# Attention stage: spread and scores as four products on 32 rows each, x loaded a unit ahead, inverse norms placed in one instruction

## The reference

```python
h = concat(patch_embedding(x), text_embedding_with_layer_norm(x_txt, ...))     # (64, 93, 192)
h = h + attn(layernorm(h));  h = h + ffn(layernorm(h))

# attn: 12 heads of 64
w = (x @ w_qkv) per head                                  # (64, 12, 93, 64)
w_normed = w / max(sqrt(sum over tokens of w*w), 1e-12)
logits = sum(w_normed * w_normed, -1) * temp              # (64, 12, 93)
Pi = softmax(logits);  Pi_norm = Pi / (sum(Pi) + 1e-8)
dots = sum over tokens of Pi_norm * (w * w)               # (64, 12, 64)
out = -(w * Pi) * 1/(1 + dots);  return out @ w_out + b_out

# ffn: 8 groups of 16 codes, 64 experts each, the best 4 are taken
z = x @ P;  scores = z @ C.T per group;  top 4, softmax over them
h = gelu(z @ W1 + b1);  yl = h @ W2 + b2;  comb = sum of yl by weight
return gelu(comb @ G1 + g1b) @ G2 + g2b
```

## Time and profile before

| | |
|---|---|
| time, median of 2 runs | 1391.95 us (1391.14 to 1392.76) |
| profiled execution | 1391.86 us, of which the span of the trace is 1390.1 us |
| stage 1, stage 2, stage 3 | 0 to 122 us, 122 to 627 us, 627 to 1390 us of the span |
| busy over the span | PE 88%, DVE 79%, ACT 78%, POOL 72% |

### The profile page before, as it was taken

One profiled execution on the slowest core, in us unless ns is written; L12 is line 12 of the kernel. 1 busy time (PEld: TensorE's weight loads), 2 busy tenths in 40 slices (PEclk: granted clock), 3 DMA queues, 4 the chain that ended last, 5 costly groups with the idle time before them and its releaser, 6 DMA issues.

```text
span 1390.1 us, 34218 instructions
## 1 busy us (share of the span) xinstructions
PE 1228.7 (88%) x12232; PEld 625.1 (45%) x12232; DVE 1104.9 (79%) x3371; ACT 1086.3 (78%) x2696; POOL 995.5 (72%) x712
## 2 busy tenths in 40 slices
PE   2953799999999999858999999999999999999996
PEld 2941466666666666522343333333343333333332
DVE  5592488888888888957888888888888888888884
ACT  0244467777677767539999999999999999999994
POOL 7641367756776676617888888888888888788884
PEclk7975899999999999969999999999999999999998
DMA  9564313222222222134214222232413323232410
GB/s 268 152 136 81 59 34 100 63 69 74 95 72 67 73 92 69 51 86 108 64 44 89 65 70 64 57 70 54 101 41 87 69 59 64 56 77 53 95 38 12
DMA packets 95705, 107.06 MB, mean 77 GB/s; under 512 B 12772, under 2 KB 92668, under 8 KB 95254
## 3 DMA queue, kind: packets, MB, share of 16 engines
q1 hardware_dynamic: 86576, 94.95, 26.3%
q10 hardware_dynamic: 6848, 6.13, 2.6%
q0 software_dynamic: 2112, 3.79, 1.1%
HBM read 67.88 MB, written 33.71 MB: 73 GB/s over the span
## 4 chain that ended last, share of the span: by engine, by line
PE 21%; ACT 18%; DVE 12%; issue 3%; POOL 0%; POOLq 0%; DVEq 0%
DVE arena L1474 11%; ACT ring L1073 11%; PE ring L1736 9%; PE code L1749 9%; ACT arena L1085 6%; PE ring L1768 2%; PE ring L1759 1%; DVE arena L1482 0%; ACT arena L1081 0%; POOL arena L817 0%; POOLq L157 0%; PE ring L1586 0%; PE ring L1634 0%; DVE arena L1257 0%; DVEq L1473 0%
## 5 line engine op out<-in xcount | busy, mean ns | idle before, releaser
L1474 DVE TENSOR_TENSOR arena<-ring,arena 128x496 f32<-128x496 f32 x1008 | 611.4, 668 | 123.4 <-ACT ring L1073 123.4
L817 POOL TENSOR_TENSOR arena<-arena 128x992 f32<-128x992 f32 x264 | 611.7, 2330 | 121.1 <-ACT arena L1085 111.6
L1073 ACT ACTIVATE ring<-ring 128x496 f32<-128x496 f32 x1008 | 544.9, 688 | 16.9 <-PE ring L1736 16.0
L1736 PE MATMUL ring<-arena,w_stack 99*32 99x496 bf16 x6144 | 423.9, 375 | 23.5 <-DVE arena L1474 17.7
L1749 PE MATMUL code<-arena,w_pad 128*32 128x496 f32 x3072 | 389.6, 581 | 8.3 <-DVE arena L1482 8.0
L1736 PEld LDWEIGHTS ring<-arena,w_stack 99*32 99x32 bf16 x6144 | 163.5, 95 | 399.6 <-DVE arena L1474 220.3
L1085 ACT ACTIVATE arena<-ring 128x992 f32<-128x992 f32 x252 | 283.9, 1127 | 0.7 <-PE ring L1736 0.7
L1578 PE MATMUL ring<-arena 96*128 96x372 f32 x384 | 135.3, 490 | 1.5 <-ACT arena L929 0.9
L1749 PEld LDWEIGHTS code<-arena,w_pad 128*32 128x32 f32 x3072 | 97.5, 110 | 59.6 <-DVE arena L1474 22.5
L753 POOL TENSOR_TENSOR arena<-arena 128x372 f32<-128x372 f32 x96 | 91.9, 986 | 32.7 <-DVE arena L1314 32.7
L1578 PEld LDWEIGHTS ring<-arena 96*128 96x128 f32 x384 | 71.7, 194 | 62.3 <-ACT arena L937 15.9
(11 more groups left out here) (143 smaller groups left out, 1437.1 us busy)
## 6 DMA issues: line engine op xcount, KB each, us to landing
arena<-gates SPq DMA_DIRECT2D x48, 496.0 KB, 6.7
gates<-arena SPq DMA_DIRECT2D x16, 744.0 KB, 11.5
arena<-h_scratch SPq DMA_DIRECT2D x32, 279.0 KB
arena<-z_parts SPq DMA_DIRECT2D x144, 62.0 KB, 2.7
h_scratch<-arena SPq DMA_DIRECT2D x16, 279.0 KB
z_parts<-arena SPq DMA_DIRECT2D x48, 93.0 KB, 2.1
arena<-h_scratch SPq DMA_DIRECT2D x12, 372.0 KB
out_h<-arena SPq DMA_DIRECT2D x12, 372.0 KB
```

The lines of the kernel that those rows point to most:

```text
L817: p_.tensor_tensor(spaces[quad % SPACES][:, j:j + 2], hid[:, POOL_DUOS.index(duo) % 2], gst[:, block // EB, j:j + 2], ALU.mult).then_inc(s ...
L1073: a_.activation(product, product, ACT.Gelu_apprx_tanh).then_inc(s_hid, 1)
L1474: v_.tensor_tensor(spaces[quad % SPACES][:, j + p], duo_bank(duo, p), gst[:, block // EB, j + p], ALU.mult).then_inc(s_gat, 1)
L1736: mm = t_.matmul(bank[32 * q:32 * q + 32], w1s[:, x + 32 * q:x + 32 * q + 32], zst[:, o, j + p], start=True, stop=True)
```

## The change

Spread and scores no longer use a block-diagonal operand of 128 rows: each becomes four products on 32 rows, one for each sequence of the unit or each pair of groups, into four different banks. `pi_placed` and `pi_scale_placed` go; pi and its inverse sum stand side by side in `pix`. Five spreads now go into the banks before DVE's first `w_pi`, which waits for all five; the sixth waits until those five have been read. w products use four banks in turn instead of two. `head_weights` is one instruction. x has two buffers and is loaded a unit earlier. The mean terms move from DVE to POOL. The lists of all five engines are written anew, with one more pass at the end for PE and ACT; the first lines of some stand in the diff, and the order at three places below it.

```diff
-        x0 = c2(ST, [SUB, D])
...
+        x0 = c2(ST, [2, SUB, D])
...
             def load_x0(u):
-                wait_apart(sp, (s_xn["A"], u))
-                sp.dma_start(x0, h0_u[u]).then_inc(s_x0, 16)
+                wait_apart(sp, (s_xn["A"], u - 1))
+                sp.dma_start(x0[:, u % 2], h0_u[u]).then_inc(s_x0[u % 2], 16)
...
             def rstd(k, u, eps):
                 wait_apart(pool, (s_mv[k], u + 1), (s_xn[k], u))
+                p_.tensor_scalar_mul(nm[k], mv[k][:, :, 0], -1.0).then_inc(s_nmean[k], 1)
                 p_.tensor_scalar_add(ve[k], mv[k][:, :, 1], eps).then_inc(s_ve[k], 1)
                 pool.wait_ge(s_ve[k], u + 1)
                 p_.tensor_tensor(rs[k], ve[k], mh2, ALU.pow).then_inc(s_rs[k], 1)
+
+            def mean_term(k, u):
+                pool.wait_ge(s_nmean[k], u + 1)
+                pool.wait_ge(s_rs[k], u + 1)
+                p_.tensor_tensor(nb[k], nm[k], rs[k], ALU.mult).then_inc(s_nb[k], 1)
...
             def pass_pool(i):
                 n2, u0, u1, u2 = i + 2, i, i - 1, i - 2
                 if has(u1):
-                    attended(u1, 0)
-                    attended(u1, 1)
...
-                src = pair0[:, c % 2, 0:UT]
+                src = ring[:, c % 4, 0:UT]
...
             def scores_copy(u, s):
-                act.wait_ge(s_sp, SUB * u + s + 1)
+                act.wait_ge(s_sp, SUB * (u + 1))
                 wait(act, s_mr, SUB * (u - 1) + s + 1)
                 wait(act, s_sd, SUB * (u - 1) + s + 1)
-                a_.copy(sc[:, s, :, 0:M], banks[2][0:ST, :].rearrange("p (a b) -> p a b", a=S)).then_inc(s_sc, 1)
+                a_.copy(sc[:, s, :, 0:M].rearrange("p (j a) b -> p j a b", j=PAIRS),
+                        ring[0:ST, 0:PAIRS, 128 * s:128 * s + 128].rearrange("p j (a b) -> p j a b", a=2)).then_inc(s_sc, 1)
...
-            def pi_placed(u):
-
-                act.wait_ge(s_pi, u + 1)
-                wait(act, s_pb, CH * u)
-                for b in range(UB):
-                    rows = slice(32 * b, 32 * b + 32)
-                    last = a_.copy(pis[rows, b, 0:N], pi[rows])
-                last.then_inc(s_pip, 1)
...
             def pass_act(i):
-                n1, u0, u1, u2, u3 = i + 1, i, i - 1, i - 2, i - 3
+                n1, u0, u1, u2, u3, u4 = i + 1, i, i - 1, i - 2, i - 3, i - 4
+                if has(u1):
+                    w_copy(u1, 3)
+                    w_copy(u1, 4)
+                    w_copy(u1, 5)
...
             def pi_made(u):
                 dve.wait_ge(s_pr, u + 1)
-                wait(dve, s_pip, u)
-                v_.tensor_scalar(pi, pe_, prc, None, ALU.mult).then_inc(s_pi, 1)
+                wait(dve, s_pb, CH * u)
+                v_.tensor_scalar(pix[:, 0:N], pe_, prc, None, ALU.mult).then_inc(s_pi, 1)
...
-                v_.reciprocal(prs, pse).then_inc(s_prs, 1)
-
-            def pi_scale_placed(u):
-                dve.wait_ge(s_prs, u + 1)
                 wait(dve, s_pb, CH * u)
-                v_.tensor_scalar(pis[:, :, N], unitsel, prs, None, ALU.mult).then_inc(s_pix, 1)
+                v_.reciprocal(pix[:, N:N + 1], pse).then_inc(s_pix, 1)
 
             def w_pi(u, c):
-                dve.wait_ge(s_pb, CH * u + c + 1)
-                pb = pair0[:, c % 2, 0:UB * (N + 1)].rearrange("p (b n) -> p b n", b=UB)
+                dve.wait_ge(s_pb, CH * u + (5 if c < 5 else 6))
+                x = (N + 1) * (c % 5)
+                pb = ring[:, 0:UB, x:x + N + 1]
...
             def head_weights(u):
                 dve.wait_ge(s_inv, u + 1)
-                for b in range(UB):
-                    last = v_.tensor_tensor(lsel[:, b, :, 0:HEADS], maskh,
-                                            inv[:, :, b:b + 1].to_broadcast([128, CH, HEADS]), ALU.mult)
-                last.then_inc(s_L, 1)
+                v_.tensor_tensor(lsel[:, :, :, 0:HEADS], maskh.unsqueeze(1).to_broadcast([128, UB, CH, HEADS]),
+                                 inv.rearrange("p c b -> p b c").unsqueeze(3).to_broadcast([128, UB, CH, HEADS]),
+                                 ALU.mult).then_inc(s_L, 1)
...
             def pass_dve(i):
-                n1, u0, u1, u2, u3 = i + 1, i, i - 1, i - 2, i - 3
-                if has(u3):
-                    top8(u3, 2)
-                if has(u0):
-                    mean_term("A", u0)
-                if has(u3):
-                    top4_shifted(u3)
+                n2, u0, u1, u2, u3 = i + 2, i, i - 1, i - 2, i - 3
...
             def w_product(u, c):
                 if c == 0:
                     pe.wait_ge(s_xt_["A"], u + 1)
-                if c < 2:
-                    wait(pe, s_rsc, CH * (u - 1) + 5 + c)
-                else:
-                    wait(pe, s_wsq, CH * u + c - 1)
-                o = pair0[:, c % 2, 0:UT]
+                if c == 0:
+                    wait(pe, s_rsc, CH * u)
+                if c >= 4:
+                    wait(pe, s_wsq, CH * u + c - 3)
+                o = ring[:, c % 4, 0:UT]
...
             def scores(u, s):
                 if s == 0:
                     pe.wait_ge(s_zf, u + 1)
-                    pe.wait_ge(s_h1, 2 * (u + 1))
-                wait(pe, s_sc, SUB * u + s)
-                t_.matmul(banks[2][0:ST, :], zf[:, ST * s:ST * s + ST], cbd, start=True, stop=True).then_inc(s_sp, 1)
+                    wait(pe, s_wsq, min(CH * (u + 3), CH * UNITS))
+                    wait(pe, s_rsc, min(CH * (u + 2), CH * UNITS))
+                for j in range(PAIRS):
+                    rows = slice(32 * j, 32 * j + 32)
+                    last = t_.matmul(ring[0:ST, j, 128 * s:128 * s + 128], zf[rows, ST * s:ST * s + ST],
+                                     cbd[rows, 128 * j:128 * j + 128], start=True, stop=True)
+                last.then_inc(s_sp, 1)
...
             def spread_pi(u, c):
                 pe.wait_ge(s_pix, u + 1)
-                pe.wait_ge(s_pip, u + 1)
-                if c < 2:
-                    pe.wait_ge(s_wsq, CH * u + 5 + c)
+                if c == 0:
+                    pe.wait_ge(s_wsq, CH * (u + 1))
+                    wait(pe, s_sc, SUB * (u - 1))
+                if c == 5:
+                    pe.wait_ge(s_rsc, CH * u + 5)
+                x = (N + 1) * (c % 5)
+                for b in range(UB):
+                    rows = slice(32 * b, 32 * b + 32)
+                    last = t_.matmul(ring[:, b, x:x + N + 1], headsel[rows, c], pix[rows], start=True, stop=True)
+                last.then_inc(s_pb, 1)
...
             def pass_pe(i):
-                u0, u1, u2, u3 = i, i - 1, i - 2, i - 3
-                if has(u3):
-                    gates_transposed(u3, 0)
-                if has(u2):
-                    out_product(u2, 1)
-                if has(u1):
-                    logits(u1)
+                u0, u1, u2, u3, u4 = i, i - 1, i - 2, i - 3, i - 4
...
```

More of the change, by code:

```diff
@@ L374, in build @@
         s_c2d = sem("attention_constants_dve")
-        s_x0, s_xr, s_xb = sem("x0_loaded"), sem("residual_loaded"), sem("residual_biased")
+        s_x0 = [sem(f"x0_loaded_{k}") for k in range(2)]
+        s_xr, s_xb = sem("residual_loaded"), sem("residual_biased")
         s_st = {k: sem(f"stats_{k}") for k in "AG"}
@@ L948, in copy_bias @@
                 wait(act, s_bd, 16 * u)
-                a_.copy(bt, pair1[:, 0, 0:UT]).then_inc(s_bt, 1)
+                a_.copy(bt, banks[2][:, 0:UT]).then_inc(s_bt, 1)
             def copy_scales(u):
@@ L953, in copy_scales @@
                 wait(act, s_rd, 16 * u)
-                a_.copy(rt, pair1[0:SUB * S, 0, UT:UT + ST]).then_inc(s_rt, 1)
+                a_.copy(rt, banks[2][0:SUB * S, UT:UT + ST]).then_inc(s_rt, 1)
             def z_copy(u):
@@ L997, in top4_exp @@
                 a_.activation(vx, vd, ACT.Exp).then_inc(s_vx, 1)
+                if u == UNITS - 1:
+                    a_.activation(psm[0:1], psm[0:1], ACT.Gelu_apprx_tanh)
             def gates_copy(u, s):
@@ L1048, in pass_act @@
-                if has(u0):
-                    pi_placed(u0)
-                if has(u2):
-                    gates_copy(u2, 2)
-                if has(n1):
-                    copy_xT("A", n1)
-                if has(u1):
-                    norm("G", u1, h1)
-                    copy_xT("G", u1)
-                    z_copy(u1)
-            for i in range(-1, UNITS + 2):
+            for i in range(-1, UNITS + 4):
                 pass_act(i)
-            a_.activation(psm[0:1], psm[0:1], ACT.Gelu_apprx_tanh)
@@ L1583, in bias @@
                 pe.wait_ge(s_gc, SUB * (u + 1))
-                wait(pe, s_lt, u + 3 if has(u + 2) else UNITS)
+                pe.wait_ge(s_h1, min(2 * (u + 3), 2 * UNITS))
                 for j in range(PAIRS):
-                    mm = t_.matmul(pair1[32 * j:32 * j + 32, 0, 0:UT], b2p[:, j], gh[:, j], start=True, stop=True)
+                    mm = t_.matmul(banks[2][32 * j:32 * j + 32, 0:UT], b2p[:, j], gh[:, j], start=True, stop=True)
                 mm.then_inc(s_bp, 1)
@@ L1680, in pass_pe @@
```

(23 more changed lines are left out.)

302 lines of the change are left out of this document (158 added, 144 removed).

## The result

The changed kernel takes 1416.9 us (median of 1410.35 and 1423.46) against 1391.95: ratio 1.019, interval 1.0154 to 1.0226. It is slower by 1.9%, where 1381 was forecast, and lies above the range. Its two runs are 13 us apart, so a gain or loss against it is known to some 7 us. The profiled execution took 1410.35 us, 18.5 more than the one of before.

| stretch | before | after | change | forecast |
|---|---|---|---|---|
| start to unit 2's w products | 182.69 | 173.57 | -9.1 | -5.0 |
| units 2 to 15 (13 units) | 366.0 | 388.9 | +22.9 | -5.9 |
| unit 15's w products to FFN | 78.4 | 84.1 | +5.7 | 0 (-5 to +5) |
| FFN | 763.0 | 761.7 | -1.3 | 0 |

The account below looks back on a forecast made before the run. The prediction took a ring of work through PE, ACT and DVE as the bound: 28.15 us a unit falling to 27.7, so -5.9 us, and -5.0 at the start, from 1391.86 to 1381 us; range 1352 to 1412.

Parts of the forecast that it names:

- Loading x a unit ahead is hidden in the steady state, where DVE never waits long for it.: Attention units: x's earlier load was to change nothing in the steady state and pay only at the start, 5.0 us.
- the other path: Attention unit, from w products over ACT's copies and squares to DVE's inverse norms: 10.7 us forecast.
- in the rest: Outcomes outside forecast and three rivals, chance 0.03; included PE's larger gaps letting the clock fall to 1.2 GHz.
- the ring: One attention unit, w products through norms, logits, softmax, spread and w times pi to the next w products: 27.4 us.
- 16.7 + 0.3: Attention unit after the norms: DVE's stretch to the last w times pi, 16.7 us, plus 0.3 for handovers.
- as forecast (about 3): Sign of a right forecast: DVE idle about 3 us a unit before the norms, waiting for ACT's squares.
- Row groups overlap: PE's spreads: four products on 32 rows run side by side, 0.21 us a spread instead of 0.72.
- rival 2: Row groups queue on PE, 0.84 us a spread: 31.8 us a unit, 1434 us in all; chance 0.13.
- The start: Before the steady units: unit 2's statistics no longer wait for x's transfer, 5.0 us less.
- The end: After unit 15's w products: the new order's extra pass priced at nothing, between -5 and +5 us.
- The prediction's own test: Signs of a wholly wrong forecast: stage clock below 0.9, or a period set by an engine outside the ring.

Follow-up runs that it names:

- fill_x0: Changed kernel plus nine unread products in PE's idle time before the w products and x loaded ahead of the store of h1: 1379.7 us, 0.992 of the kernel before.
- fill_gap: Changed kernel plus nine products whose result nobody reads in PE's idle time before the w products: 1406.7 us, ratio 1.0102 to the kernel before.
- stats_later: Changed kernel plus the nine products before the w products, with x's statistics moved behind negated attention and third mark on DVE: 1379.0 us, ratio 0.9921.
- x0_early: Changed kernel with x's load one pass earlier on SP's queue, ahead of the store of h1 and the residual's load: 1401.8 us, ratio 1.0074.
- fill_else: Changed kernel plus the same nine products placed where PE waits for z's copy and the head weights, away from the w products: 1423.4 us, ratio 1.0227.
- row128_x0: Changed kernel with x loaded early and each spread and scores product on all 128 rows instead of 32, result left wrong: 1453.5 us, ratio 1.044.
- before_x2: Kernel before with one part of the change alone, x in two buffers: 1386.2 us, ratio 0.9953.

## Why the prediction was wrong

**The step that failed first: "Loading x a unit ahead is hidden in the steady state, where DVE never waits long for it."** That read DVE's waits under the old order of two lists. The change also turned SP's list, so that x's load comes after the residual's, and moved the statistics ahead of the negated attention, the third mark and the norms. Counted as the other path was: issue 3.9 us before the w products, landing 12.0 later, statistics 0.9, small steps and mark 2 us, so the norms 11 us after the w products instead of 10.7, and behind the negated attention POOL, the out products and the residual, back to the load: a ring of 30 us. The 12 us are in no row ahead of the prediction. The nearest in the old trace is unit 2's load, issued here and waited for until 149.18, 8.8 us:

```profile
140.41 0.24 SPq L558 DMA_DIRECT2D arena<-h_scratch  x1
```

With 8.8 for 12.0 the ring is an estimated 27 us, level with the forecast's 27.7 and no ground for calling the load hidden. That this ring holds the unit is shown by fill_x0 against fill_gap (27 us) and by stats_later, which opens that ring at another place.

**The second: the clock, put "in the rest" with 0.03 for all others.** I argued from the share of a whole unit, 79% busy. What is left idle lies just before the w products, and the first of them is on the ring: 1.45 us to the first copy became 2.9. Shown by fill_x0 against x0_early (22 us), and by fill_else, where the same work elsewhere did nothing. The Trainium skill, "TensorE: Matmul & The Clock Gate", section HAM oscillation, describes a case of this: waits for transfers between groups of products bring the clock down, and each next group starts slow. The trace agrees on the slow start, 5.33 us for 2.67; but the waits here are on other engines and shorter than the page's, none over 1.3 us in the unit shown, and the measurement decides. A fall of the clock should have been a rival with a price: 1.45 us and the slower products behind it, together 2.5 (norms 13.0 us after the w products in the unit shown, 351.04 to 364.08, and 10.5 in fill_x0), 13 x 2.5 = 33 us.

**What held, once both were removed.** In fill_x0 the unit is what the forecast had: 27.37 us against 27.7. That the whole comes so near, 1379.7 us against 1381, is in part luck: units 2 to 15 brought 10.2 us instead of 5.9, and the end took back 3.9. The norms come 10.53 us after the w products (forecast 10.7), and the rest takes 16.9 (16.7 + 0.3). DVE there:

```profile
344.27 0.86 DVE L1225 BATCH_NORM_STATS2 arena<-arena 124x6 f32<-124x192 f32 x3
...
350.28 0.18 DVE L1329 TENSOR_SCALAR arena<-arena 128x24 f32<-128x24 f32 x1 [3.17 <-ACT arena L951]
...
350.83 0.46 DVE L1337 TENSOR_TENSOR arena<-arena 128x288 f32<-128x288 f32 x1
```

It waits 3.17 us for ACT's squares, as forecast (about 3). The head weights in one instruction take 0.46 us against 0.45. In the changed kernel the same instruction took 1.14 (365.27 above), with POOL's step after its six products running beside it (365.19 to 366.09), which x's late landing had pushed there. The Trainium skill, "SBUF — State Buffer", section SBUF: two separate sides, says that a VectorE instruction with two SBUF inputs, as this one has, and a GpSimd instruction that reads SBUF exclude each other on one port pair; the two durations agree with that, and no run here tested it alone.

**Row groups overlap**: 0.26 us a spread against 0.21 taken; rival 2 with 0.84 was wrong for this kernel. Made to happen in row128_x0, it gave 31.57 us a unit against 31.8 in that rival's working, so the place and the price were right. Of the two statements of the Trainium skill that were weighed there ("TensorE: Matmul & The Clock Gate", on LDWEIGHTS and on packing small matmuls), the trace bears out the second, that loads overlap products of other row groups: eight passes in 0.26 us, where eight on all rows take 0.94. PE is busy 22.9 us in an undisturbed unit of x0_early, against 21.8.

**The start**: the second buffer alone brought more than the 5.0 us. From unit 0's first w product to unit 2's it is 56.4 us in the kernel before (126.32 to 182.69), 49.3 in before_x2 and 49.5 in the changed kernel, 7.0 less. The other 2 us of the table's 9.1 lie ahead of unit 0, which begins anywhere from 124.1 to 127.6 us in the runs here. As a whole before_x2 gained 5.7, since its units 2 to 15 took 1.7 us longer. **The end**, priced at nothing because the extra pass "holds only a bias and a scales transpose" (PE has one more pass, ACT two), cost 5.7 in the changed kernel and 3.9 in fill_x0 (614.74 - 532.41 against 78.4). Some 3 us of either can be read in the traces: the last bias copy on ACT waits 4.8 to 4.9 us for the store of the bias before it, which SP's new list issues behind the first loads of the FFN, and PE idles 3.7 to 3.8 us ahead of the FFN instead of 0.8. No run tested this, and the rest wasn't taken apart.

The prediction's own test named the failure: "a granted clock below 0.9 in the stage, or a period set by an engine outside this ring". The stage mean was 0.91, the w products at 0.50, and the second ring is such a period.

## What to carry to other kernels

When a change takes a full engine down, look where its new idle time will lie and what stands right behind it: work at the head of a ring may then be done at the lower clock, and a mean busy share doesn't show it. When a load gets a second buffer, follow its queue's list, not its buffer: a load behind one that waits for the end of the unit is itself issued at the end of the unit. Two causes that hold the unit at nearly one length hide each other, so neither fix alone shows its worth (10 and 15 us, together 37).

## What the runs showed that I had not expected

Nine products whose result nobody reads, 2 us of PE's time a unit, made the kernel 22 us faster once x was early. PE's idle time of 1.3 to 1.5 us ahead of the w products went before the lower clock in some units and not in others of one execution (x0_early). Four row groups that write to four banks run a spread's eight passes in 0.26 us; on 128 rows they take 0.94.
